# All inputs on one DMA queue in the order of their use, gates and router weights in one packed transfer

## The reference

```python
def _L0_xattn_ref(x, weight):
    xq = quant_dequant_act_1x128(x)             # one scale for each token and 128 features
    wq = quant_dequant_weight_128x128(weight)   # one scale for each 128x128 block
    return jnp.einsum('emk,enk->emn', xq, wq)

def _L0_ffn_ref(x, gate_w, shared_gate_w, wg, wu, wd, swg, swu, swd):
    probs = softmax(x @ gate_w.T)
    top_w, top_i = jax.lax.top_k(probs, 4)      # weights divided by their sum, scattered to comb
    y = jnp.einsum('eti,ehi->eth', silu(x wg) * (x wu), wd)
    moe_out = jnp.einsum('te,eth->th', comb, y)
    sh = silu(x @ swg.T) * (x @ swu.T) @ swd.T
    return moe_out + sigmoid(x @ shared_gate_w.T) * sh

x = x + tanh(g_xattn) * _L0_xattn_ref(layernorm(x), ctx_2048)
x = x + tanh(g_ffn) * _L0_ffn_ref(layernorm(x), ...)
```

## Time and profile before

| what | value |
|---|---|
| three timed runs | 213.73, 213.79 and 211.87 us, median 213.73 |
| profiled execution, first to last instruction | 209.8 us |
| timed runs beside that span | 2.1 to 4.0 us longer |
| mean granted TensorE clock | 0.976 of full |
| instructions | 2493 |
| bytes moved | 9.94 MB |

### The profile page before, as it was taken

The page is one execution under the profiler, slowest core; times in us unless marked ns, Lnnn a source line. Parts: engine busy times, 40 slices in busy tenths (PEclk is TensorE's granted clock), DMA queues, the critical chain, the costliest instruction groups (busy, mean ns, idle before and its releaser), DMA issues.

```text
span 209.8 us, 2493 instructions
## 1 busy us (share of the span) xinstructions
PE 170.3 (81%) x743; PEld 127.9 (61%) x743; DVE 144.5 (69%) x284; ACT 100.6 (48%) x216; POOL 90.9 (43%) x99
## 2 busy tenths in 40 slices
PE   0101494998999875999995998799999999999993
PEld 0001254775777444777773876577777777788871
DVE  0789886797888889869888678756435544355573
ACT  2183343375588322655444558335553355434550
POOL 5152443424535766335344324243455334543520
PEclk9999997599999999699999999999999999999999
DMA  5877777300000000000000000002000000000002
GB/s 152 300 257 226 207 200 215 119 0 5 0 0 0 0 2 0 3 2 0 0 3 0 0 0 0 0 3 100 2 0 0 0 0 0 0 0 0 2 0 100
DMA packets 4494, 9.94 MB, mean 47 GB/s; under 512 B 1001, under 2 KB 1001, under 8 KB 4484
## 3 DMA queue, kind: packets, MB, share of 16 engines
q1 hardware_dynamic: 4340, 9.30, 14.0%
q10 hardware_dynamic: 144, 0.52, 1.0%
HBM read 8.78 MB, written 1.05 MB: 47 GB/s over the span
## 4 chain that ended last, share of the span: by engine, by line
PE 48%; DVE 35%; ACT 7%; issue 5%; DMA 3%; POOL 2%; ACTq 0%; DVEq 0%; POOLq 0%
PE bank L974 43%; DVE act L764 4%; ACT a_hi L423 3%; DVE silu L756 3%; DVE a_lo L769 3%; DVE xc L650 3%; DMA x<-xs 3%; DVE y L694 2%; PE bank L1010 2%; DVE bn L575 2%; DVE x L684 2%; DVE xe L642 2%; DVE xe L604 2%; DVE xq L651 2%; DVE ce L604 2%
## 5 line engine op out<-in xcount | busy, mean ns | idle before, releaser
L275 POOL TENSOR_TENSOR w_lo<-w_raw,w_hi 128x512 fp32r<-128x512 f32 (+1 forms) x34 | 43.5, 1281 | 69.6 <-ACT w_hi L409 69.6
L974 PE MATMUL bank<-h_hi,w_hi 128*128 128x512 f32 x132 | 53.8, 408 | 3.4 <-DVE silu L756 3.4
L974 PE MATMUL bank<-h_hi,w_lo 128*128 128x512 f32 x132 | 52.0, 394 | 0.0
L974 PE MATMUL bank<-h_lo,w_hi 128*128 128x512 f32 x132 | 51.8, 392 | 0.0
L423 ACT ACTIVATE a_hi<-act 128x512 fp32r<-128x512 f32 (+1 forms) x34 | 21.5, 633 | 59.6 <-DVE act L764 59.4
L769 DVE TENSOR_TENSOR a_lo<-act,a_hi 128x512 fp32r<-128x512 f32 (+1 forms) x34 | 24.3, 713 | 23.1 <-ACT a_hi L423 23.1
L756 DVE TENSOR_TENSOR silu<-silu,bank 128x512 f32<-128x512 f32 (+1 forms) x33 | 22.5, 684 | 20.6 <-PE bank L974 20.1
L280 POOL TENSOR_TENSOR w_lo<-w_raw,w_hi 128x256 fp32r<-128x256 f32 (+1 forms) x34 | 26.6, 783 | 17.2 <-ACT w_hi L413 17.1
L974 PE MATMUL bank<-a_hi,w_hi 128*128 128x512 f32 (+1 forms) x68 | 31.1, 457 | 3.7 <-DVE a_lo L769 3.7
L974 PEld LDWEIGHTS bank<-h_hi,w_hi 128*128 128x128 f32 x132 | 25.0, 190 | 9.8 <-DVE silu L756 4.9
L974 PEld LDWEIGHTS bank<-h_hi,w_lo 128*128 128x128 f32 x132 | 25.0, 189 | 5.6
(11 more groups left out here) (109 smaller groups left out, 189.4 us busy)
## 6 DMA issues: line engine op xcount, KB each, us to landing
w_raw<-w_full SPq DMA_DIRECT2D x16, 384.0 KB, 3.6
x<-xs SPq DMA_DIRECT2D x4, 256.0 KB, 5.3
out_t<-fin SPq DMA_DIRECT2D x4, 256.0 KB, 2.1
cw<-ctx_t ACTq DMA_DIRECT2D x1, 512.0 KB, 5.7
cw<-ctx_t SPq DMA_DIRECT2D x1, 512.0 KB, 6.6
w_raw<-w_last SPq DMA_DIRECT2D x1, 256.0 KB, 3.1
spread<-sel SPq DMA_DIRECT2D x1, 111.4 KB
gate_raw<-gate_t SPq DMA_DIRECT2D x1, 10.0 KB, 5.5
```

What stands on the lines that cost most here:

```text
L275: nc.gpsimd.tensor_tensor(w_lo[:, slot, 0:cols], w_raw[:, bass.ds(c, 1), 0:cols], w_hi[:, slot, 0:cols].bitcast(F32), ALU.subtract).then_i ...
L974: last = nc.tensor.matmul(out, w[k][a], x_of[k][b], start=(start and k == 0 and i == 0), stop=(stop and k == blocks - 1 and i == 2))
```

## The change

The first half of `ctx` is issued on SP behind `x` of batch 0 in place of ScalarE. The two gates and the router weights come in one array `small` of 22 values for each partition, built on the host, and land in `small_in`. ScalarE's tanh reads it there. The router weights are copied from it into the zeroed `gate_raw` by GpSimd (`place_gate_w`). The order on SP is now x0, ctx0, x1, small, weights 0 and 1, selector, x2, ctx1, x3, and then the other weights.

```diff
--- before.py
+++ after.py
@@ -50,7 +50,7 @@
 AX = mybir.AxisListType
 
 
-def flamingo_gated_block(nc, xs, ctx_t, g_x, g_f, gate_t, w_full, w_last, sel, out_t):
+def flamingo_gated_block(nc, xs, ctx_t, small, w_full, w_last, sel, out_t):
     with ExitStack() as stack:
         def sb(name, shape, dt=F32):
             return stack.enter_context(nc.sbuf_tensor(name, shape, dt))
@@ -90,7 +90,7 @@
         diag = sb("diag", [CB, HALVES, 2 * CB])
         scl_c = sb("scl_c", [P, HALVES, 2 * CB])
         deq = sb("deq", [P, TILES, KC, 2])
-        g_raw = sb("g_raw", [P, 2])
+        small_in = sb("small_in", [P, 2 + KC * GP])
         g_tanh = sb("g_tanh", [P, 2])
 
         gate_raw = sb("gate_raw", [P, KC, P])
@@ -141,14 +141,14 @@
 
         x_landed = [sem(f"x_landed{b}") for b in range(B)]
         ctx_landed = [sem(f"ctx_landed{h}") for h in range(HALVES)]
-        gates_landed = sem("gates_landed")
-        gate_w_landed = sem("gate_w_landed")
+        small_landed = sem("small_landed")
         sel_landed = sem("sel_landed")
         w_landed = [sem(f"w_landed{i}") for i in range(2)]
         stored = sem("stored")
 
         consts, ident_filled = sem("consts"), sem("ident_filled")
         gate_zeroed, spread_zeroed = sem("gate_zeroed"), sem("spread_zeroed")
+        gate_placed = sem("gate_placed")
         tanh_done, gate_hi_done, gate_split = sem("tanh_done"), sem("gate_hi_done"), sem("gate_split")
         dve_did, pool_did = sem("dve_did"), sem("pool_did")
 
@@ -203,25 +203,30 @@
             def load_x(b):
                 sp.dma_start(x[:, tile_slice(b), :], xs[:, tile_slice(b), :]).then_inc(x_landed[b], 16)
 
-            load_x(0)
-            load_x(1)
-            sp.wait_ge(gate_zeroed, 1)
-            sp.dma_start(gate_raw[:, :, 0:GP], gate_t).then_inc(gate_w_landed, 16)
-            sp.dma_start(g_raw[:, 0:1], g_x.to_broadcast((P, 1))).then_inc(gates_landed, 16)
-            sp.dma_start(g_raw[:, 1:2], g_f.to_broadcast((P, 1))).then_inc(gates_landed, 16)
-            load_x(2)
-            load_x(3)
-            sp.dma_start(cw[:, batches(1)], ctx_t[:, batches(1)]).then_inc(ctx_landed[1], 16)
-            sp.wait_ge(spread_zeroed, 1)
-            sp.dma_start(spread[0:3 * G, 0:ROWS], sel).then_inc(sel_landed, 16)
-
-            for c in range(UNITS):
+            def load_ctx(h):
+                sp.dma_start(cw[:, batches(h)], ctx_t[:, batches(h)]).then_inc(ctx_landed[h], 16)
+
+            def load_w(c):
                 if c >= 2:
                     sp.wait_ge(w_landed[c % 2], 16 * (c // 2))
                 if c < FULL:
                     sp.dma_start(w_raw[:, c, :], w_full[c]).then_inc(w_landed[c % 2], 16)
                 else:
                     sp.dma_start(w_raw[:, c, 0:GUL + D], w_last).then_inc(w_landed[c % 2], 16)
+
+            load_x(0)
+            load_ctx(0)
+            load_x(1)
+            sp.dma_start(small_in[:], small).then_inc(small_landed, 16)
+            load_w(0)
+            load_w(1)
+            sp.wait_ge(spread_zeroed, 1)
+            sp.dma_start(spread[0:3 * G, 0:ROWS], sel).then_inc(sel_landed, 16)
+            load_x(2)
+            load_ctx(1)
+            load_x(3)
+            for c in range(2, UNITS):
+                load_w(c)
             for n in range(HALVES * KC):
                 h, k = n // KC, n % KC
                 sp.wait_ge(fin_done, n + 1)
@@ -246,6 +251,12 @@
             nc.gpsimd.memzero(comb_parts[:]).then_inc(consts, 1)
             nc.gpsimd.memzero(spread[:]).then_inc(spread_zeroed, 1)
 
+            def place_gate_w():
+                pool.wait_ge(small_landed, 16)
+                pool.wait_ge(gate_zeroed, 1)
+                nc.gpsimd.tensor_copy(gate_raw[:, :, 0:GP], small_in[:, 2:].rearrange("p (k g) -> p k g", k=KC))\
+                    .then_inc(gate_placed, 1)
+
             def inverse_std(which, b, var_sem, rstd_sem):
 
                 pool.wait_ge(var_sem, b + 1)
@@ -288,6 +299,7 @@
 
             inverse_std(0, 0, var_ready, rstd_ready)
             inverse_std(0, 1, var_ready, rstd_ready)
+            place_gate_w()
             add_magic(0)
             subtract_magic(0)
             add_magic(1)
@@ -335,7 +347,6 @@
 
         @block.scalar
         def _(a):
-            a.dma_start(cw[:, batches(0)], ctx_t[:, batches(0)]).then_inc(ctx_landed[0], 16)
             a.preload_act_table(ACT.Exp)
 
             def centre(b):
@@ -444,13 +455,13 @@
             scale_x(0)
             centre(1)
             scale_ctx(1)
-            a.wait_ge(gates_landed, 32)
-            nc.scalar.activation(g_tanh[:], g_raw[:], ACT.Tanh).then_inc(tanh_done, 1)
+            a.wait_ge(small_landed, 16)
+            nc.scalar.activation(g_tanh[:], small_in[:, 0:2], ACT.Tanh).then_inc(tanh_done, 1)
             scale_x(1)
             copy_xqt(0)
             copy_xqt(1)
             residual0(0)
-            a.wait_ge(gate_w_landed, 16)
+            a.wait_ge(gate_placed, 1)
             nc.scalar.activation(gate_hi[:], gate_raw[:], ACT.Copy).then_inc(gate_hi_done, 1)
             weights(0, 0, 0, first=True)
             residual0(1)
@@ -1156,7 +1167,9 @@
 
     ctx_t = np.ascontiguousarray(a["ctx_2048"].reshape(B, D, KC, P).transpose(3, 0, 2, 1))
     gate = np.concatenate([a["L0_ffn_gate_w"], a["L0_ffn_shared_gate_w"], np.zeros((GP - G, D), np.float32)])
-    gate_t = np.ascontiguousarray(gate.reshape(GP, KC, P).transpose(2, 1, 0))
+    gate_t = gate.reshape(GP, KC, P).transpose(2, 1, 0).reshape(P, KC * GP)
+    g_pair = np.broadcast_to(np.concatenate([a["g_xattn"], a["g_ffn"]])[None, :], (P, 2))
+    small = np.ascontiguousarray(np.concatenate([g_pair, gate_t], axis=1))
 
     gw = np.concatenate([a["L0_ffn_wg"].reshape(E * EI, D), a["L0_ffn_swg"]])
     uw = np.concatenate([a["L0_ffn_wu"].reshape(E * EI, D), a["L0_ffn_swu"]])
@@ -1176,8 +1189,7 @@
     owner = np.concatenate([np.repeat(np.arange(E), EI), np.full(SI, E)])
     sel = np.ascontiguousarray(np.tile(np.eye(G, dtype=np.float16)[:, owner], (3, 1)))
 
-    arrays = {"xs": xs, "ctx_t": ctx_t, "g_x": a["g_xattn"], "g_f": a["g_ffn"], "gate_t": gate_t,
-              "w_full": w_full, "w_last": w_last, "sel": sel}
+    arrays = {"xs": xs, "ctx_t": ctx_t, "small": small, "w_full": w_full, "w_last": w_last, "sel": sel}
     nc = bacc.Bacc("TRN2", target_bir_lowering=False, num_devices=1)
     args = [nc.dram_tensor(n, v.shape, mybir.dt.from_np(v.dtype), kind="ExternalInput").ap() for n, v in arrays.items()]
     out_t = nc.dram_tensor("out_t", (KC, P, T), F32, kind="ExternalOutput").ap()
```

## The result

The changed kernel took 214.20 us in the median of 20 executions (213.51 to 214.78), the kernel before 213.19 (211.87 to 214.24). The ratio is 1.0045, with a 95% interval of 1.0026 to 1.0064. It is a small loss, where a gain of 1.3 us was forecast; the forecast of 212.4 was itself made against a median of 213.73 from three runs. Each ratio in this document leaves out executions over 1.5% above the fastest of the same kernel, which here are mostly those with a low mean clock.

What follows compares the result with a forecast made beforehand. The prediction took the load of `x` at the start to bind, only the first 7.5 us being open to gain. Part 1's 1.3 us, all else 0, gave 213.73 - 1.3 = 212.4 us; forecast 211.8 to 213.2, range with rivals 210.2 to 214.2.

Steps and rivals of the forecast that it cites:

- Where the change acts: Loads: only the first 7.5 us, up to the maximum of `ctx`, can gain; nothing later can be won directly.
- Part 1: `ctx` behind `x` on SP: maximum of `ctx` starts at 6.15 at most, not 7.46; gain 1.3 us (0.5 to 1.9).
- ctx0 is complete at 5.25 and lands at 6.05: First half of `ctx` on SP: 786 kB moved by 5.25 us, plus a lag of 0.8 (0.2 to 1.7).
- Part 4: Weights 0 and 1 and selector ahead of x2, ctx1, x3 on SP: over 20 us of cover, price 0.
- Part 2: Three small loads on SP become one, behind ctx0 and x1: nothing on the path gains.
- Part 3: GpSimd's copy of the router weights before `cw`'s first sum: 0.1 to 0.2 us, covered, price 0.
- The fast single queue: Rival: loads on SP run at 338 to 405 GB/s from 2.5 us, gain 2.0 to 2.3 us; chance 0.11.
- The clock rival: TensorE's half-speed stretch from 34.4 to 41.2 us is missed in most runs, giving 210.5 us; chance 0.18.
- the slower rival: ctx0 lands after 7.46 us: 0.3 to 0.9 lost, 214.0 to 214.6, 216.5 with an extra half-speed stretch; chance 0.09.
- named signs of being wrong: Maximum still at 7.4 or later; early shift lost by 50 us to half clock; TensorE waiting for weights or x2.
- 3.9 us outside the span: Time outside the profiled span of 209.8 us against the median of 213.73, taken as untouched by the change.

Runs made afterwards that it cites:

- places alone: The kernel before with the gates' array widened from 2 to 22 columns, so the arrays behind it lie 64 bytes further: 214.71 us, ratio 1.0050.
- places restored: The changed kernel with `small_in` put behind all other SBUF arrays, so every other array lies where it lay before: 213.02 us, ratio 0.9993.
- before_ctx_on_sp: The kernel before with only the first half of `ctx` issued on SP behind x0, old places in SBUF: 212.28 us, ratio 0.9946.
- hold_weights: The changed kernel at old places, with weights 0 and 1 and all behind them issued only after ctx0 landed: 212.10 us, ratio 0.9892.
- hold_x1_too: `hold_weights` with the second part of `x` also issued only after the first has landed: 212.29 us, ratio 0.9994.

## Why the prediction was wrong

- *Where the change acts* ("nothing later can be won directly"): right for the loads, wrong as a bound on loss. The step that failed is the unspoken one that all work after 7.5 us keeps its pace, and that the widened array costs nothing. It cost 1.1 us, from 141 us to the end, shown by places alone and by places restored, and it lies in the products that read `h_hi` and `h_lo`. The program was at hand and its addresses could have been read; no row of the trace of before would have priced them.
- *Part 1, x lands at 4.0 and its statistics end at 5.3*: it landed at 4.74. *ctx0 is complete at 5.25 and lands at 6.05*: complete at 5.2 + (786 - 686)/261 = 5.6, landed at 6.98, with a lag of 1.4, inside its range and not at its value of 0.8. Two terms were mis-sized. The rate, 259 GB/s taken for a queue behind which other bytes had come to stand, was 204; that is 0.3 us of the 0.9 by which `ctx` is late. The lag is the other 0.6. With the order alone, `before_ctx_on_sp`, 780 kB had moved by 5.2 us as forecast, the lag was 1.1, and the gain was 1.15 of the forecast 1.3.
- *Part 4, weights ahead of x2, price 0*: right for the readers of x2 and ctx1, wrong for the loads in front. I asked who waits for what is moved back and not what the bytes moved forward take from those ahead. Price 0.2 to 0.8 us of start (6.71 and 7.01 against 6.47, 8.12 against 7.32).
- *Part 2, tiny loads, no gain on the path*: their issues of 0.63 us each had in fact kept the following loads away from the awaited ones. This is argued from the issue times, since no kernel kept them and moved the weights; in `hold_weights` and `hold_x1_too` a wait takes their place.
- *Part 3, the copy at no cost*: right. It took 0.36 us where 0.1 to 0.2 was said, and the sum behind it still started 0.47 earlier.
- *The fast single queue*: did not happen; 204 GB/s. The Trainium skill, DMA: Bandwidth & Descriptors, "Issuing engines are not separate DMA queues", says that a second issuing engine saves only the time of issuing. The traces agree: with late weights, 235 to 240 GB/s on one queue and 229 to 259 on two, from 2.5 to 5.0 us.
- *The clock rival*: the mechanism was right, and as a rival it named only the gain, a half-speed stretch missed; one more of them stands only at the far end of the slower rival. The changed kernel met more such stretches in its profile (1.6 us). That the change makes them likelier is not shown: 15 of its 20 executions were at 0.965 to 0.968, of before 15 of 35, 9 of 11 and 7 of 17 in three jobs.
- *The slower rival* named ctx landing after 7.46. It landed at 6.98. The loss had another cause, which no rival named. Nor did any of the named signs of being wrong come: the early shift was still there at 115 us, and TensorE waited for no weights.
- *3.9 us outside the span*: it is 2.1. A fast execution's profile was set against the median of all; the forecast of 1.3 did not depend on it, but the base did.

The sum as measured: -0.45 at the start and +1.1 from the pace make +0.65; the two kernels' medians differ by 1.0, and spans at like clock by 0.6 (212.1 against 211.5, from different jobs). The mix of clocks could hold the rest of the 1.0; before's clocks beside the changed kernel are not listed, so that stays open.

## What to carry to other kernels

Put nothing behind an awaited load until it has landed, unless it is needed soon: a wait on the issuing queue was worth 0.2 to 0.8 us of the start here. Holding back `x1` as well won another 0.4 of the start and no time that the runs show. When an array changes its size, keep the others where they were (put the new one last) and compare the pace of a steady stretch before and after; otherwise a change to one thing is a change to two. Compare executions at the same granted clock where its dips come and go. `hold_weights`, the changed kernel with both repairs, beat both kernels: at like clock 1.3 us under before (three executions) and 1.8 under the change (from different jobs). `before_ctx_on_sp`, which moves the load of `ctx` and nothing else, is within 0.2 us of it (210.5 against 210.3), so no gain from the packed load is shown.

## What was not expected of the hardware

- Moving some arrays of SBUF by 64 or 128 bytes against the others slowed TensorE's steady run of float32r products from 18 in 4.12 us to 18 in 4.15 to 4.20, at full clock. Moving all by 64 did not. The loss is in the 12 products that read `h_hi` or `h_lo` (2.74 us to 2.81), and 0.03 to 0.04 of it comes even where neither of their operands has moved.
- Loads queued behind a load on the same queue delayed it (`x` landed at 6.9 in place of 6.1), and the whole rate from 2.5 to 5.0 us was 204 to 220 GB/s with them and 229 to 259 without.
- The same program ran at 208.3 to 212.3 us, mostly by how many half-speed stretches it met: the same pause of TensorE, 2.5 us with 0.93 us of work around it, brought one in one execution and none in another.
